# Group norm folded into per-image stem weights, taken in five sets of images, and the level 0 maxima moved to the second stage

## What is computed

```python
def _gn(v, G=32, eps=1e-05):            # 32 groups of 8 channels
    g = v.reshape(B_, G, C_ // G, H_, W_)
    m = jnp.mean(g, axis=(2, 3, 4), keepdims=True)
    s = jnp.var(g, axis=(2, 3, 4), keepdims=True)
    return ((g - m) / jnp.sqrt(s + eps)).reshape(v.shape)

x_aux = silu(conv1x1(_gn(x), w_sta, b_sta))          # the stem: 256 -> 128 channels
for _ in range(3):
    y1.append(0.9 * maxpool5x5(y1[-1]) + 0.1 * sumpool5x5(y1[-1]) / 25)
    y2.append(sumpool5x5(e * y2[-1]) / (sumpool5x5(e) + 1e-6))     # e = exp(y2[-1] - max over the batch)
...
x = x + silu(conv(y * a))                            # more convolutions on y1 and y2
x = x + attention(_gn(x), w1, w2)
```

## Time and profile before

| | |
|---|---|
| median of 3 runs | 1384.13 us (1377.48 to 1387.42) |
| the profiled execution | 1376.88 us, span 1375.1 us |
| PE busy | 1206.2 us, 88% of the span |
| DVE busy | 1152.7 us, 84% |
| ACT busy | 726.0 us, 53% |
| POOL busy | 293.6 us, 21% |
| mean granted TensorE clock | 0.96 |

### The profile page before, as it was taken

One profiled execution on the slowest core, in us unless ns is written; L12 is line 12 of the kernel. 1 busy time (PEld: TensorE's weight loads), 2 busy tenths in 40 slices (PEclk: granted clock), 3 DMA queues, 4 the chain that ended last, 5 costly groups with the idle time before them and its releaser, 6 DMA issues.

```text
span 1375.1 us, 17821 instructions
## 1 busy us (share of the span) xinstructions
PE 1206.2 (88%) x6730; PEld 1026.1 (75%) x6730; DVE 1152.7 (84%) x1220; ACT 726.0 (53%) x781; POOL 293.6 (21%) x247
## 2 busy tenths in 40 slices
PE   3559898766899999999899999999998999999697
PEld 1249898655678877877788788878887887797597
DVE  7779887799989889989998999899989977985343
ACT  0246667663375447536753675366546643853342
POOL 1566767401111111111111111111111111000000
PEclk9769999987999999999999999999999999999899
DMA  7403123253665566566456644764475466001000
GB/s 287 168 31 93 77 86 115 97 126 90 142 143 118 151 177 122 113 169 160 107 121 197 141 109 108 208 140 104 116 200 126 108 144 157 0 1 62 0 0 31
DMA packets 72303, 159.91 MB, mean 116 GB/s; under 512 B 33088, under 2 KB 35904, under 8 KB 72256
## 3 DMA queue, kind: packets, MB, share of 16 engines
q0 software_dynamic: 23904, 92.11, 29.9%
q1 hardware_dynamic: 47648, 66.85, 14.7%
q10 hardware_dynamic: 704, 0.30, 0.1%
HBM read 41.46 MB, written 25.17 MB: 48 GB/s over the span
## 4 chain that ended last, share of the span: by engine, by line
PE 36%; DVE 18%; issue 17%; ACT 6%; DMA 3%; DVEq 0%; POOL 0%; ACTq 0%; POOLq 0%
PE slot L1299 12%; PE slot L1246 10%; PE ps_level L1299 10%; DVE between L1574 4%; PE slot L1315 3%; DVE a L1574 2%; DMA boxes<-twos 2%; DVE pt_all L345 1%; ACT a L1478 1%; ACT between L1428 1%; DVE f_all L410 1%; DVE x L1617 1%; ACT f_all L1447 1%; ACT a L1428 1%; DVE tall L323 1%
## 5 line engine op out<-in xcount | busy, mean ns | idle before, releaser
L1299 PE MATMUL ps_level<-v_all,pt_all 128*128 128x256 f32 x1536 | 200.1, 287 | 13.6 <-DVE pt_all L1578 8.2
L1299 PEld LDWEIGHTS ps_level<-v_all,pt_all 128*128 128x128 f32 x1536 | 189.6, 192 | 17.3 <-DVE pt_all L1578 15.8
L1299 PE MATMUL slot<-f_all,q_all 128*128 128x512 f32 x768 | 189.7, 397 | 0.0
L1574 DVE SCALAR_TENSOR_TENSOR a<-between,k_columns,a 128x992 f32<-128x992 f32 (+1 forms) x128 | 157.6, 1232 | 6.9 <-ACT a L1428 4.6
L1299 PEld LDWEIGHTS slot<-f_all,q_all 128*128 128x128 f32 x768 | 140.1, 188 | 27.9
L1578 DVE TENSOR_TENSOR pt_all<-slot,pt_all 128x1024 fp32r<-128x1024 f32 x64 | 78.2, 1221 | 40.8 <-ACT pt_all L1442 40.6
L1451 ACT CAST v_all<-y 128x1024 fp32r<-128x1024 f32 x32 | 33.8, 1055 | 134.6 <-DVE y L1607 134.4
L1456 ACT ACTIVATE mixed<-ps_level,row_inv 128x256 f32<-128x256 f32 x64 | 30.2, 473 | 133.5 <-PE ps_level L1299 133.5
L1428 ACT ACTIVATE a<-between,k_columns 128x1024 f32<-128x1024 f32 x64 | 79.3, 1240 | 33.3 <-DVE between L1574 32.3
L1607 DVE SCALAR_TENSOR_TENSOR y<-slot,k_columns,y 128x1024 f32<-128x1024 f32 x32 | 40.9, 1282 | 57.0 <-PE slot L1246 55.1
L1574 DVE SCALAR_TENSOR_TENSOR between<-y,k_columns,between 128x992 f32<-128x992 f32 x64 | 78.8, 1249 | 7.8 <-ACT between L1428 6.6
(11 more groups left out here) (204 smaller groups left out, 2752.1 us busy)
## 6 DMA issues: line engine op xcount, KB each, us to landing
levels<-x_all SPq DMA_DIRECT2D x32, 512.0 KB, 2.6
boxes<-twos POOLq DMA_DIRECT2D x28, 543.0 KB, 4.8
boxes<-twos POOLq DMA_DIRECT2D x28, 527.0 KB, 4.6
x_all<-in_x SPq DMA_DIRECT2D x8, 1024.0 KB, 12.8
f_all<-levels SPq DMA_DIRECT2D x8, 1024.0 KB, 7.4
x<-in_x SPq DMA_DIRECT2D x8, 1024.0 KB, 5.9
out<-x SPq DMA_DIRECT2D x8, 1024.0 KB, 4.1
twos<-boxes POOLq DMA_DIRECT2D x14, 561.0 KB, 3.0
```

The source lines that it names most:

```text
L1299: last = nc.tensor.matmul(out, lhs, rhs, start=(n == 0), stop=(n == len(parts) - 1))
L1574: nc.vector.scalar_tensor_tensor(o, u, keep["taps"][:, s, c, tap:tap + 1], o, ALU.mult, ALU.add).then_inc(taps.sem, 1)
```

## The change

Four things change, all in front of the third stage.

- **Stem.** `xn` and `normalise` are gone. ACT scales the stem's weights by `rstd` per image (`weigh`, two tiles of 128 x 128 per image, into `w_image`), PE multiplies `w_sta` by `shift` (`biases`, one or two columns), ACT adds `b_sta` (`bias`), and `silu` takes the result as its bias. `convolve` reads `x_all` directly. The statistics are taken in five sets of images (`SETS`) in place of two of four, with their pieces placed between the other work of each engine. POOL's box sum steps are placed between its five powers.
- **Weights.** The six raw weights have tiles of their own (the last one lies in `work_b`), and are loaded behind the images with no wait. The three small loads of the stem go to the head of SP's queue.
- **Level 0 of image 0.** Its seven `maxima` steps and its mixture move from the first stage to s = -1 and s = 0 of the second; all later chain steps of that stage stand one s later, and `WHOLE` moves by one tile. ACT's copy of level 1 (`zero_next`) moves from the end of the first stage to s = 0.
- **PE** runs 16 products of 128 x 128 with no use (`keep_warm`) at the end of the first stage.

The core of the diff:

```diff
-STAGED = {"w1": (0, 1, 0, 512), "w2": (0, 1, 512, 1024), ...}
+SETS = ((0,), (1,), (2, 3), (4, 5), (6, 7))
+    def zero_first(self, first):
+        self.nc.scalar.copy(self.zero[:, :, 2:2 + W], first).then_inc(self.zeroed.sem, 1)
 @block.sync
+            sp.dma_start(keep["group"][:, :], consts["group"]).then_inc(sta_in, 16)
+            sp.dma_start(w_sta[:, :, :], rows("sta")).then_inc(sta_in, 16)
+            sp.dma_start(keep["columns"][:, :], w["columns"]).then_inc(sta_in, 16)
             for i in range(B):
                 sp.dma_start(x_all[:, i], x_v[i]).then_inc(x_in[i], 16)
+            sp.dma_start(keep["ident"][:, :], consts["ident"]).then_inc(ident_in, 16)
             sp.dma_start(box_raw[:, :], consts["box"]).then_inc(box_in, 16)
-            def load_weights(k):
-                sp.wait_ge(xn_done, STAGED[k][1] * CT)
...
+            for k in SPLIT:
+                sp.dma_start(raw(k), rows(k)).then_inc(weights_in[k], 16)
 @block.scalar
+            def weigh(g):
+                act.wait_ge(rstd_done, g + 2)
+                for n in SETS[g]:
+                    for t in range(CT):
+                        at = n * CT + t
+                        nc.scalar.activation(w_image[:, n, t], w_sta[:, t], ACT.Copy, scale=rstd[:, at:at + 1]).then_inc(weighted_done, 1)
+            def bias(g):
+                act.wait_ge(bias_sum_done, g + 1)
+                nc.scalar.activation(b_image[:, part], ps_bias[:, part], ACT.Identity, bias=keep["b_sta"]).then_inc(bias_done, 1)
             def silu(n):
+                act.wait_ge(bias_done, SET_OF[n] + 1)
                 act.wait_ge(sta_done, n + 3)
-                nc.scalar.activation(x_all[:, n, 0], ps[:, n % 2], ACT.Silu, bias=keep["b_sta"]).then_inc(stem_done, 1)
+                nc.scalar.activation(x_all[:, n, 0], ps[:, n % 2], ACT.Silu, bias=b_image[:, n:n + 1]).then_inc(stem_done, 1)
 @block.tensor
+            def biases(g):
+                pe.wait_ge(shift_done, g + 1)
...
+            def convolve(n, h):
+                if h == 0:
+                    pe.wait_ge(weighted_done, CT * n + CT)
+                    pe.wait_ge(stem_done, n + 1)
...
+            keep_warm(nc, keep, ps_warm[:, 0:P], 16)
 @block.vector
-            def normalise(n):
...
+            add_eps(4)
+            maximum(4)
+            shifts(4)
+            for n in range(5, B):
+                maximum(n)
-WHOLE = frozenset([*range(1, 7), *range(11, 17)])
+WHOLE = frozenset([*range(2, 8), *range(12, 18)])
 second stage, scalar
-                if s == 9:
-                    chain.zero_next(act, 2)
+                if s in (0, 10):
+                    chain.zero_next(act, 1 if s == 0 else 2)
 second stage, vector
+                if s < 0:
+                    chain.maxima(dve, 0, 0, 0, 1, 2)
                 if s + 1 < total:
                     product(s + 1)
+                if s == 0:
+                    chain.maxima(dve, 0, 0, 3, 4)
...
+                if s == 0:
+                    chain.maxima(dve, 0, 0, 5, 6)
+                    chain.mixture_of_sums(dve, 0)
-                if 0 <= s < 7:
-                    chain.maxima(dve, 0, 1, s)
+                if 1 <= s < 8:
+                    chain.maxima(dve, 0, 1, s - 1)
```

268 lines of the change are left out of this document (156 added, 112 removed).

## The result

| | before | after |
|---|---|---|
| median of the runs, us | 1381.86 (1377.33 to 1387.45, 12 runs) | 1366.98 (1360.58 to 1373.60, 12 runs) |
| profiled execution, us | 1376.88 (span 1375.1) | 1360.91 (span 1359.1) |
| first stage, to DVE's first `tile_max` | 89.5 | 59.6 |
| second stage, to the end of the last `divide` | 175.3 | 187.4 |
| third stage, the rest of the span | 1110.4 | 1112.2 |

The ratio is 0.9885, with an interval of 0.9860 to 0.9909. So the kernel is 14.9 us faster by the medians and 16.0 us by the profiled executions. 1363 had been forecast, with 1348 to 1374 around it; the gain was put at 21.3 us. The time is only 4 us off where the gain is 6.4 short, because the forecast started from the median of three runs (1384.1) and the kernel before came to 1381.9 over twelve.

A forecast was written before the change was run, and what follows sets the result against it. The first stage was taken as bound by DVE's normalisations and statistics with PE waiting, the second paced by DVE. -27.8 us there and +6.5 in the second gave -21.3, from 1384.1 to 1363 us, range 1348 to 1374.

The forecast's parts named there:

- Stage one, rebuilt: First stage: the new order followed from the front ends at 61.4 us in place of 89.15, a gain of 27.8 us.
- half an image at low clock: First stage's end: after PE idles some 2.3 us, convolutions 6 and 7 take 3.4 + 1.7 + 3.4 us, ending at 57.7.
- The lower bound of the gain: First stage: smallest gain, put at 21 us of a range 21 to 34, for dear powers and more low-clock images.
- Waits it adds: First stage: late weight loading and level stores hold nothing up; first split due at 40 us, last image near 28.
- Fill: First stage's end on PE: 16 useless products take 3.7 us, and the next stage's first turn shrinks from 1.91 to about 1.0.
- Stage two, the front: Start of the second stage: eight added DVE instructions and a new ACT wait cost a net +6.5 us.
- Shifting `WHOLE` and the later steps by one s: 0, DVE sets the pace: Second stage: moving the later steps one s keeps their number, and DVE sets the pace, so the cost is 0.
- The bound of +12.5: Second stage: upper bound of its added cost, with five maxima steps at 2.82 us each beside POOL.
- The clock did not stay low: Rival 1, first stage: PE's clock stays at half rate through the stem, gain 6, cost 6.5, total 1384 us; chance 7%.
- images weren't late: Rival 4, first stage: late images keep DVE's statistics the bound, some 15 us more waits, about 1378 us; chance 2%.
- Stage one gave more than I counted: Part of rival 2: more is hidden, first stage gains 34 us, second costs 4, total 1354 us; chance 20%.
- Rival 3: Second stage: moved maxima meet POOL and stretch to 4.42 us, losing more than the first stage gains; 1401 us; chance 3%.

The follow-up runs named there:

- zero_later: Changed kernel with ACT's copy of level 1 at s = 1 in place of s = 0; second stage 184.4 us, ratio to the kernel before 0.9882.
- paired_step4: steps_paired with level 0's maxima step 4 also moved behind divide(0); second stage 186.3 us, ratio to the kernel before 0.9922.
- no_fill: Changed kernel without the 16 keep_warm products; first two stages 246.9 us, ratio to the kernel before 0.9902.
- steps_paired: Changed kernel with level 1's maxima steps 0 and 1 both at s = 1, later steps mostly back in place; second stage 178.9 us, ratio 0.9880.
- level2_back: Changed kernel with level 1's mixture, level 2's steps and WHOLE's second half one s earlier; second stage 182.6 us, ratio to the kernel before 0.9846.
- step4_late: Changed kernel with level 0's maxima step 4 behind divide(0) in place of ahead of residual(0); second stage 183.7 us, ratio 0.9876.
- before_again: The kernel before, profiled again with no edit; first two stages repeat within 0.1 us, third stage 6.8 us longer.
- maxima_in_first: New stem, but level 0's maxima in the first stage's tail and the kernel before's second stage; stages 67.0 and 175.1 us, ratio 0.9873.
- three_steps_early: level2_back with level 0's maxima steps 0 to 2 in the first stage, the rest one place earlier; stages 62.1 and 181.8 us, ratio 0.9858.

## Why the prediction was right or wrong, point by point

**Stage one, rebuilt: right, 27.8 forecast and 29.9 measured.** Of the chain's steps the first convolution came at 14.95 (14.9), the last power was done at 44.4 (44.7), and the power took 0.70 us for two columns and 1.01 for four (0.75 and 1.0). The fill took 3.73 (3.7). The one that didn't come in this execution is "half an image at low clock" for convolution 6: PE stood idle for 1.9 us in front of it, and yet 16 records took 7.11 us, so PE ended its convolutions at 55.7 and not 57.7. That is the 2 us by which the gain was too small. In zero_later and paired_step4, with the same code, it did come (8.81 us), and their gains were 28.8 and 27.7: whether the term comes is a matter of chance. The lower bound of the gain was summed wrong: the dear power (2.7) and two images at low clock (7) together give 18 us and not 21, while on the upper side both terms had been taken.

**Waits it adds: right.** The weights' late loading held nothing up; the low parts ended at 58.3 (59.2 forecast).

**Fill: right in size, without worth.** It holds the start back by 0.9 us and gives 0.8 back in the second stage (no_fill). I had counted its end at 61.4 into the gain of one stage and 0.5 us for the clock into the other, and so had it at a small loss.

**Stage two, the front: right in sum, by luck.** 6.5 us by tile 1, as summed (5.0 to 6.3 in the other executions with these steps). Steps 0 to 2 were covered (forecast +0.2; the product of tile 1, the second behind them, even began 0.5 us earlier than before, 7.9 for 8.4 us into the stage). Steps 3 and 4 were counted at 1 and cost 3.8, as both met POOL, 3.46 and 3.36 us. Steps 5 and 6 and the mixture met nobody, 3.8 for 4.7. The ACT wait was 2.05 for 2.1. Against them stands level 1's first step, which met POOL before, took 2.82 us and left these tiles, where 1 was counted. So an error of 2.8 us in one term was made up by smaller ones in the others.

**"Shifting `WHOLE` and the later steps by one s: 0, DVE sets the pace": wrong, and this is the step that failed.** It cost 5.6 us behind tile 1. At the boundary behind tile 7, step 6 of level 1 landed in front of the maximum on which the whole next level waits: 11.0 us there and 8.7 in steps_paired, 1.6 net of what that step costs one tile earlier. The rest arises behind tile 8. level2_back, which undoes the shift of level 1's mixture, level 2 and the second half of `WHOLE`, takes 4.8 us away. That the whole 4.8 are the price of this shift is not shown, since zero_later and step4_late took 3.0 and 3.7 us away without touching it. What is shown is that the term isn't 0: with nearly all of the shift undone the stage takes 178.9 and 179.8 us in place of 187.4. My reason didn't carry: what DVE has to do isn't fixed. A step costs between 1.2 and 3.4 us, by how much of a POOL instruction is in front of it, and shifting changes that at each tile. The bound of +12.5 held the measured 12.1 by luck: it was made for the five steps in front. The range of the time had even taken a cost of 11 at most. It held because stage one gave more.

**The third stage: carried over at 1110.5, measured 1112.2.** before_again shows that 7 us there need no cause in the code, so the sign of being wrong, a third stage off by more than 5 us, was set too narrow. What this means for the medians is open. An estimate: a run's time less its span is 1.8 us; if I take that and the first two stages of the profile from the medians, the third stage is 1115 us in before, 1118 in after, and 1122 and 1126 in the two measurements of steps_paired. By it, 2.9 of the 6.4 us that the gain fell short lie in the third stage and 3.5 in the first two. steps_paired's front is 7 to 8 us shorter than after's and its ratios aren't lower. Its third stage took 1114.9 us in one profile and 1123.1 in the other; before had 1110.4 and 1117.2, and the other changed kernels 1112.2 to 1122.4. Whether an earlier start favours the longer periods or the samples are too few wasn't settled.

**The rivals.** The clock did not stay low (1.00 in the stage, 3.7 us for eight records from the third image on; 0.94 in the worst executions of the same code), and images weren't late. Stage one gave more than I counted, but stage two cost more. Rival 3, the maxima that meet POOL, was right in mechanism and too large in price: it took 3.5 us of stretch where I asked for 21; paired_step4 shows its locked form, at 1.4 us for each tile. The Trainium skill (SBUF — State Buffer, section "SBUF: two separate sides") says that a shared port pair is held exclusively for a whole instruction by whichever of a GpSimd operation that reads SBUF and a DVE operation with two SBUF inputs starts first. The timelines agree to about a tenth of a us: DVE's steps end 1.08 and 1.16 us behind POOL's instruction (1.2 alone), POOL's ends 2.23 behind DVE's step (2.36 alone). In the prediction I had used a weaker form of it, "contention", as an upper bound, and so priced steps by a mean. Whether the clock made the second stage longer is a rival that I hadn't listed. Its granted clock was 0.95 before and 0.91 after, but 0.91 to 0.92 also in the two profiles of the paired kernel (178.9 and 179.8 us) and 0.93 in paired_step4 (186.3), so the stage's length doesn't follow it.

**The move as a whole.** It lost: 12.3 for 7.5 us beside the new stem, 11.8 for 9.5 with the old one. The kernel gained in spite of it. Only with the old stem does the whole time show the loss (1.0039, an interval above 1); beside the new one the ratios 0.9873 and 0.9885 can't be told apart.

## What to carry to other kernels

DVE steps with two SBUF inputs don't have one price beside a POOL that works in the same loop: count 1.2 us plus what is left of POOL's instruction when the step starts. Here that was up to 3.5 us beside an instruction of 2.4, and 4.48 beside one of about 4.5 (maxima_in_first). Put such steps where DVE waits anyway (here the tail of the stem), and not in front of the reduction on which the next level waits. "It is only shifted by one tile" is a change to be priced like any other, and edits that each save 3 to 5 us need not add, since each decides the meetings anew. Where a kernel's stages have such meetings, or a clock that falls in some executions, one profile on the mark doesn't prove a term of the sum.

## What the runs showed of the hardware that I had not expected

- The meeting of DVE and POOL can turn on less than the trace resolves: with POOL's recorded start 0.02 us ahead DVE waited in after and POOL in three_steps_early. It costs DVE up to 2.2 us beside a POOL instruction of 2.4, and it can repeat tile by tile: 3.3 us for each step over five tiles in paired_step4, POOL ahead by 0.11 to 0.18 us each time. It takes tiny operations as well: a multiplication of 128x4 on DVE took 1.87 us beside POOL in the first stage of after, where others of that size took 0.16. Reductions of 128x1024, which have one input, stayed at 1.2 us throughout.
- POOL's power costs 0.70 us for 2 columns, 1.01 for 4 and 1.64 for 8.
- The same program had, in the same place of five images, a granted clock of 1.00 in one execution and 0.57 to 0.59 in another, with 131 or 133 us for an image. The clock can also fall or not at a pause of the same length: 16 records took 7.11 or 8.81 us behind 1.9 us of idle PE.
